# Self attention of a perceiver block: heads scored in row tiles of 32 rows, two heads sharing their output rows, the norm of q and k by query tile with GpSimd, half of the first output product early

## The reference

```python
x = x + cross(layernorm(x), ctx) @ W_out.T
h = layernorm(x)
q, k, v = split(h @ w_qkv.T + b_qkv)            # 16 heads of 16 columns each
q = q * rsqrt(mean(q * q) + 1e-6) * qn_w        # for each head
k = k * rsqrt(mean(k * k) + 1e-6) * kn_w
attn = softmax(q @ k.T / 4)                     # for each head, 256 x 256
x = x + (attn @ v) @ w_proj.T + b_proj
```

## Time and profile before

| | |
|---|---|
| median of 3 runs | 748.99 us (747.96 to 749.51) |
| the profiled execution | 750.28 us |
| its span, first to last instruction | 748.6 us |
| mean granted TensorE clock | 0.963 |
| TensorE products busy | 646.4 us (86%), 4972 instructions |
| TensorE weight loads busy | 390.7 us (52%) |
| VectorE busy | 413.4 us (55%) |
| ScalarE busy | 464.5 us (62%) |
| GpSimd busy | 71.9 us (10%) |

### The profile page before, as it was taken

How to read it: one execution, slowest core, us unless ns; L and a number is a source line. 1 busy time by engine, 2 the same in 40 slices (tenths; PEclk the granted TensorE clock), 3 DMA queues, 4 the chain that set the end, 5 groups by cost and what they waited for, 6 DMA issues and landing times. The chain is left out here.

```text
span 748.6 us, 14468 instructions
## 1 busy us (share of the span) xinstructions
PE 646.4 (86%) x4972; PEld 390.7 (52%) x4972; DVE 413.4 (55%) x903; ACT 464.5 (62%) x558; POOL 71.9 (10%) x148
## 2 busy tenths in 40 slices
PE   1698777878788769898589999999999899988997
PEld 1354444444445345575235555555555567754886
DVE  6576352231322315865578898988883426446443
ACT  3899969999999974472036676767767046303100
POOL 3010201000100003000110101111110200000000
PEclk9999979999999999999758999999999999999899
DMA  5787765384433114000802332323230740000000
GB/s 132 217 245 212 232 205 168 105 239 152 143 112 109 49 25 151 1 1 0 287 9 72 86 81 76 88 79 84 77 83 2 241 139 1 2 0 1 0 1 14
DMA packets 52694, 73.39 MB, mean 98 GB/s; under 512 B 10866, under 2 KB 29618, under 8 KB 52658
## 3 DMA queue, kind: packets, MB, share of 16 engines
q1 hardware_dynamic: 51890, 72.19, 33.0%
q10 hardware_dynamic: 768, 0.73, 0.3%
HBM read 58.89 MB, written 12.85 MB: 96 GB/s over the span
## 5 line engine op out<-in xcount | busy, mean ns | idle before, releaser
L1575 DVE TENSOR_REDUCE sb_m_blk<-ps 128x1 f32<-128x512 f32 x256 | 159.6, 683 | 22.8 <-PE ps L1432 21.7
L1383 ACT ACTIVATE sb_probs<-ps 128x1024 f32<-128x1024 f32 x128 | 125.9, 1025 | 52.9 <-PE ps L1462 51.7
L651 ACT ACTIVATE sb_probs<-ps 128x1024 f32<-128x1024 f32 x128 | 124.0, 1016 | 16.5 <-PE ps L697 14.2
L655 ACT ACTIVATE sb_probs<-sb_probs,sb_neg_cap,sb_cap 128x4096 f32<-128x4096 f32 x32 | 121.6, 3801 | 1.1
L714 PE MATMUL ps<-sb_probs,sb_v_st 128*32 128x256 f32 x1024 | 77.5, 400 | 41.1 <-ACT sb_probs L655 38.7
L1432 PE MATMUL ps<-sb_k_st,sb_q_m 96*128 96x512 bf16 x256 | 91.4, 402 | 2.7 <-DVE sb_m_blk L1575 2.0
L697 PE MATMUL ps<-sb_q_st,sb_k_st 112*128 112x256 bf16 x512 | 76.6, 285 | 5.9 <-DMA sb_k_st<-k_parts_l 4.2
L1462 PE MATMUL ps<-sb_q_st,sb_k_st 115*128 115x256 bf16 x512 | 77.7, 275 | 1.4 <-ACT sb_probs L1383 1.4
L697 PEld LDWEIGHTS ps<-sb_q_st,sb_k_st 112*128 112x128 bf16 x512 | 46.2, 101 | 49.7 <-ACT sb_probs L651 23.8
L1478 PE MATMUL ps<-sb_probs,sb_v_st 128*32 128x256 f32 x1024 | 67.7, 385 | 0.2 <-ACT sb_probs L1383 0.2
L714 PEld LDWEIGHTS ps<-sb_probs,sb_v_st 128*32 128x32 f32 x1024 | 24.2, 110 | 70.4 <-ACT sb_probs L655 49.3
(11 more groups left out here) (264 smaller groups left out, 875.0 us busy)
## 6 DMA issues: line engine op xcount, KB each, us to landing
sb_k_st<-k_parts_l SPq DMA_DIRECT2D x223, 64.0 KB, 2.0
sb_k_st<-k_parts_l SPq DMA_DIRECT2D x93, 128.0 KB, 3.2
k_parts_l<-sb_v_proj SPq DMA_DIRECT2D x24, 256.0 KB
k_parts_l<-sb_early SPq DMA_DIRECT2D x48, 128.0 KB
sb_v_proj<-ctxT_blocks SPq DMA_DIRECT2D x8, 512.0 KB, 8.9
sb_early<-ctxT SPq DMA_DIRECT2D x7, 512.0 KB, 4.0
sb_v_rows<-ctx_by_pair SPq DMA_DIRECT2D x7, 512.0 KB, 3.9
sb_k_st<-k_parts_l SPq DMA_DIRECT2D x64, 32.0 KB, 1.8
```

The lines of the kernel that those rows point to most:

```text
L651: a.activation(probs[:, j % 2, 4 * g:4 * g + 4, :], scores_bank(g), ACT.Tanh).then_inc(s["tanh"], 1)
L655: a.activation(probs[:, j % 2], probs[:, j % 2], ACT.Exp, bias=k.neg_cap[:, 0:1], scale=k.cap[:, 0:1]).then_inc(s["exp"], 1)
L1383: sc.activation(probs[:, g], scores_bank(g), ACT.Exp).then_inc(s["exp"], 1)
L1575: v.tensor_reduce(k.m_blk[:, b, q, blk:blk + 1], k.ps[:, m_bank(m_turn_of(idx)), :], AX.X, ALU.max).then_inc(s["m_read"], 1)
```

## The change

Five parts, and what follows from them.

1. In `stage_cross0`, before the last value products, TensorE turns the first half of `o_nat` and multiplies it by the first half of the weights; VectorE copies the turned half. The stage after does the second half only and adds to the same banks. The ternary weights' absolute sum goes from the self attention to VectorE's list here. Two `keep_busy` products of 256 columns are added.
2. q and k are handled for each query tile by itself (bias, square, sum, product). GpSimd multiplies by the norm weights beside the chain. The ternary scaling goes ahead of the bias on VectorE, the second mask row behind the squares on ScalarE.
3. A head's scores use the 32 rows that hold it and its neighbour. `q_par` holds q twice, once with the odd heads' rows zero and once with the even heads' (two masked copies instead of sixteen). A pair is now heads h and h + 2, in different row tiles, and their scores go to different banks.
4. In `v_self` odd heads fill columns 16 to 31 and even heads columns 0 to 15, and both add to the same 32 output rows (`joined`), so the result fills one bank, and the output product goes over two blocks.
5. `w_proj0` is loaded in one transfer, without zero rows; the memset for them and SyncE's wait for it go.

```diff
@@ stage_cross0: tensor, vector
                 body(it, False)
+            pe.wait_ge(s["o_read"], H - 1)
+            for q in range(QT):
+                last = t.transpose(k.ps[:, 4, q * P:(q + 1) * P], k.o_nat[:, q, 0:P], k.ident[:, :])
+            last.then_inc(k.sem("a_oT_ps"), 1)
+            pe.wait_ge(k.sem("a_oT"), 1)
+            pe.wait_ge(s["v_copied"], H)
+            pe.wait_ge(k.sem("w2_in"), 16 * W2_LOADS)
+            for q in range(QT):
+                t.matmul(k.ps[:, 6 + q, 0:D], k.oT[:, 0, q * P:(q + 1) * P], k.w_out0[:, 0, :], start=True, stop=False)
             for c in range(4):
                 pv(H // 2 - 1, 3, c, False)
+            keep_busy(k, 1, 1, D)
             sel(H - 1, 1)
+            keep_busy(k, 1, 1, D)
...
+            dve.wait_ge(k.sem("a_oT_ps"), 1)
+            v.tensor_copy(k.oT[:, 0, :], k.ps[:, 4, 0:S]).then_inc(k.sem("a_oT"), 1)
+            dve.wait_ge(k.sem("w2_in"), 16 * W2_LOADS)
+            v.tensor_reduce(k.w_sum[:, :], k.w_ffn0[:, :, :].rearrange("p t n -> p (t n)"), AX.X, ALU.add,
+                            apply_absolute_value=True).then_inc(k.sem("c_w_sum"), 1)
             copy_acc(H - 1, 1)
@@ Small
+    def edges(self, h, c, tiles):
+        return c == 0 and not (self.joined and h % 2), c == tiles - 1 and not (self.joined and h % 2 == 0)
@@ stage_self0
-    att = Small(k, H, False,
-                q_of=lambda h, q: k.q_mask[:, h, q * P:(q + 1) * P],
-                k_of=lambda h, nk: k.kT_self[:, h // 8, 0:nk],
+    quad = lambda h: slice(32 * (h // 2 % 4), 32 * (h // 2 % 4) + 32)
+    att = Small(k, [((h, h + 2), q) for h0 in range(0, H, 4) for q in range(QT) for h in (h0, h0 + 1)], False,
+                q_of=lambda h, q: k.q_par[quad(h), h % 2, h // 8, q * P:(q + 1) * P],
+                k_of=lambda h, nk: k.kT_self[quad(h), h // 8, 0:nk],
                 v_of=lambda h, c: k.v_self[:, c, h, :],
...
+                out_of=lambda h, q, r: k.ps[quad(h), 4, h // 8 * S + q * P:h // 8 * S + (q + 1) * P],
+                scores=lambda n: k.ps[:, 2 * (n % 2):2 * (n % 2) + 2, 0:S],
+                turned=lambda n: k.ps[:, 6 + n % 2, :], joined=True)
@@ stage_self0: gpsimd (behind the two memsets, which stay)
+            for q in range(QT):
+                pool.wait_ge(k.sem("b_qk_rows"), q + 1)
+                heads = lambda a: a[:, q, :].rearrange("p (s h d) -> p s h d", s=2, d=DH)
+                nc.gpsimd.tensor_tensor(heads(k.qk_w), heads(k.qk), k.w_qkn[:, :, :].unsqueeze(2).to_broadcast([P, 2, H, DH]),
+                                        ALU.mult).then_inc(k.sem("b_qk_w"), 1)
@@ stage_self0: tensor
-            update_pe(k, pe, "a", k.oT, KT, k.w_out0, True)
+            for q in range(QT):
+                last = t.transpose(k.ps[:, 0, q * P:(q + 1) * P], k.o_nat[:, q, P:2 * P], k.ident[:, :])
+            last.then_inc(k.sem("a_oT_ps"), 1)
+            keep_busy(k, 1, 1, D)
+            pe.wait_ge(k.sem("a_oT"), 2)
+            for q in range(QT):
+                last = t.matmul(k.ps[:, 6 + q, 0:D], k.oT[:, 1, q * P:(q + 1) * P], k.w_out0[:, 1, :], start=False, stop=True)
+            last.then_inc(k.sem("a_y"), 1)
+            keep_busy(k, 5, 1)
...
+            keep_busy(k, 3, 6)
             for q in range(QT):
+                pe.wait_ge(k.sem("b_qkn"), q + 1)
...
+            keep_busy(k, 1, 7, D)
+            pe.wait_ge(k.sem("b_qkT_in"), 3)
+            pe.wait_ge(k.sem("b_v_in"), 2)
             small_pe(k, pe, att)
-            update_pe(k, pe, "b", k.oT_pad, 4, k.w_proj0, False, norm=False)
+            update_pe(k, pe, "b", k.oT, KT, k.w_proj0, False, norm=False)
@@ stage_self0: scalar
             act.wait_ge(k.sem("d_mask_in"), 16)
+            mask_rows(0)
             for q in range(QT):
+                act.wait_ge(k.sem("b_qk_rows"), q + 1)
+                sc.activation(k.qk_sq[:, q, :], k.qk[:, q, :], ACT.Square).then_inc(k.sem("b_sq"), 1)
+            mask_rows(1)
             act.wait_ge(k.sem("b_qkT"), 1)
-            for h in range(8, H):
-                sc.activation(k.q_mask[:, h, :], k.ps[:, 2, 0:S], ACT.Copy, scale=k.head_mask[:, h - 8:h - 7]).then_inc(k.sem("b_qm_act"), 1)
+            sc.activation(k.q_par[:, 0].rearrange("p c q -> p (c q)"), k.ps[:, 0, :], ACT.Copy, scale=k.par_mask[:, 0:1]).then_inc(k.sem("b_qkT_in"), 1)
@@ stage_self0: vector, behind the copy of the turned rows
+            vec.tensor_scalar(k.w_qkn[:, 0, :], k.w_qkn[:, 0, :], 1.0 / np.sqrt(DH), None, ALU.mult).then_inc(k.sem("b_w"), 1)
+            dve.wait_ge(k.sem("c_w_total"), 1)
...
+            for q in range(QT):
+                dve.wait_ge(k.sem("b_qk"), q + 1)
+                vec.tensor_tensor(k.qk[:, q, :], k.ps[:, 3 + q, :], k.b_qkv0[:, 0:2 * D], ALU.add).then_inc(k.sem("b_qk_rows"), 1)
+            for q in range(QT):
+                dve.wait_ge(k.sem("b_sq"), q + 1)
+                link(vec.tensor_reduce(k.rs_v[:, 2 * H * q:2 * H * (q + 1)], k.qk_sq[:, q, :].rearrange("p (h d) -> p h d", d=DH), AX.X, ALU.add))
+            link(vec.tensor_scalar(k.rs_v[:, :], k.rs_v[:, :], 1.0 / DH, 1e-6, ALU.mult, ALU.add))
+            rsqrt(k, link, 64)
+            for q in range(QT):
+                dve.wait_ge(k.sem("b_qk_w"), q + 1)
+                vec.tensor_tensor(heads(k.qk), heads(k.qk_w), k.rs_y[:, 2 * H * q:2 * H * (q + 1)].unsqueeze(2).to_broadcast([P, 2 * H, DH]),
+                                  ALU.mult).then_inc(k.sem("b_qkn"), 1)
...
-            for h in range(8):
-                vec.tensor_scalar(k.q_mask[:, h, :], k.ps[:, 0, 0:S], k.head_mask[:, h:h + 1], None, ALU.mult).then_inc(k.sem("b_qm_dve"), 1)
+            dve.wait_ge(k.sem("b_qkT_in"), 2)
+            vec.tensor_scalar(k.q_par[:, 1].rearrange("p c q -> p (c q)"), k.ps[:, 0, :], k.par_mask[:, 1:2], None, ALU.mult).then_inc(k.sem("b_qkT_in"), 1)
...
-            vec.tensor_copy(k.oT_pad[:, :, :].rearrange("p (b g) q -> p b (g q)", b=2), k.ps[:, 4:6, :]).then_inc(k.sem("b_oT"), 1)
+            vec.tensor_copy(k.oT[:, :, :].rearrange("p c q -> p (c q)"), k.ps[:, 4, :]).then_inc(k.sem("b_oT"), 1)
```

More of the change, by code:

```diff
@@ L987, in scores @@
     def scores(n):
-        h0, q = a.pairs[n]
+        heads, q = a.pairs[n]
         nk = a.tiles(q) * P
@@ L991, in scores @@
             pe.wait_ge(s["exp"], 2 * (a.base + n - 1))
-        for e in range(2):
-            o = k.ps[:, n % 2, e * S:e * S + nk]
-            last = t.matmul(o, a.q_of(h0 + e, q), a.k_of(h0 + e, nk), start=True, stop=not a.causal)
+        for e, h in enumerate(heads):
+            o = a.scores(n)[:, e, 0:nk]
+            last = t.matmul(o, a.q_of(h, q), a.k_of(h, nk), start=True, stop=not a.causal)
             if a.causal:
@@ L999, in turn @@
     def turn(n):
-        h0, q = a.pairs[n]
+        q = a.pairs[n][1]
         pe.wait_ge(s["pn"], 2 * (a.base + n + 1))
@@ L1043, in copy_turned @@
         sc.activation(k.sp_T[:, n % 2, :].rearrange("p (e m) -> p e m", e=2)[:, :, 0:nk],
-                      k.ps[:, 2 + n % 2, :].rearrange("p (e m) -> p e m", e=2)[:, :, 0:nk], ACT.Copy).then_inc(s["PT_copied"], 1)
-    for n, (h0, q) in enumerate(a.pairs):
+                      a.turned(n).rearrange("p (e m) -> p e m", e=2)[:, :, 0:nk], ACT.Copy).then_inc(s["PT_copied"], 1)
+    for n, (_, q) in enumerate(a.pairs):
         nk = a.tiles(q) * P
@@ L1051, in small_act @@
         for e in range(2):
-            sc.activation(k.sp_rows[:, n % 2, e, 0:nk], k.ps[:, n % 2, e * S:e * S + nk], ACT.Exp,
+            sc.activation(k.sp_rows[:, n % 2, e, 0:nk], a.scores(n)[:, e, 0:nk], ACT.Exp,
                           bias=k.nmax[:, 2 * n + e:2 * n + e + 1],
@@ L1185, in _ @@
[L1185 to L1192 removed]
+            dve.wait_ge(k.sem("a_oT_ps"), 2)
@@ L1671, in stage_self1 @@
     v, sc, t = nc.vector, nc.scalar, nc.tensor
-    causal = Small(k, 2 * E_T, True,
+    by_two = lambda heads: [((h, h + 1), q) for h in range(0, heads, 2) for q in range(QT)]
+    one_bank = lambda n: k.ps[:, n % 2, :].rearrange("p (e m) -> p e m", e=2)
+    turned = lambda n: k.ps[:, 2 + n % 2, :]
+    causal = Small(k, by_two(2 * E_T), True,
                    q_of=lambda h, q: k.e_qT[:, h // 2, q * P:(q + 1) * P],
```

122 lines of the change are left out of this document (53 added, 69 removed).

## The result

The change made the kernel slower: 758.94 us, median of 4 runs (754.69 to 761.31), against 748.76 before (4 runs, 747.96 to 749.51); ratio 1.0127, 95% interval 1.0085 to 1.017: a small loss, but clear of the noise. The profiled execution took 757.73 us, its span 756.0. The forecast was 738.2. What came true is the rival called *Slower*, which had been priced at 761 and given a chance of 0.03.

What follows compares the result with a forecast made beforehand. TensorE was taken to bound the head loop, a chain hopping between engines the run-up. Terms +0.4 + 0 - 6.7 + 1.2 + 0.4 - 3.9 - 2.2 = -10.8 on the 748.99 median gave 738.2 us; range 735.0 to 742.5.

Steps and rivals of the forecast that it cites:

- Slower: Rival for the head loop: clock stays at 0.5, period 3.2, 761 us if for all sixteen pairs; chance 0.03.
- Part 1: Early half of the first output product: value products 0.4 us late (+0.4); the norm waits for GpSimd's memset, so gain 0.
- Port free: Rival at the norm's start: the 1.01 us tensor_scalar isn't waiting for the memset; 733.1 us; chance 0.10.
- Part 2: From the turned rows' copy to the first scores: 18.25 us shrinks to 11.55, -6.7 us.
- The clock: Half-clock losses before the first scores: +1.2 us at the qkv products, +0.4 (0 to 1.2) for the later gap.
- Part 3: Head loop: paired scores overlap (-0.43), tile-shape switch costs 0.15; period 2.06 becomes 1.79, -3.9 us in all.
- Scores one after another: Rival for the head loop: the two row tiles don't overlap, loop +2.1, 744.2 us; chance 0.10.
- Partial overlap: Rival for the head loop: only the middle two records overlap, three slots for four, loop -1.0, 741.1 us; chance 0.08.
- Part 4: Behind the loop: smaller copy (-0.5) and eight output-product records instead of sixteen (-1.7), -2.2 us.
- a loop at 0.5: Sign that would show the forecast wrong: the head loop running at a granted clock of 0.5.
- 25 us as the point from which it decides: Head loop: half clock, +1.4 us a period, decides the result once it lasts over some 25 us.

Runs made afterwards that it cites:

- e6: e1 with the 3 x 8192 memset moved from GpSimd to ScalarE at the block's start; 733.8 us, ratio 0.9798 to the kernel before.
- e7: e6 without the early half of the first output product; 740.4 us, ratio 0.9904 to the kernel before.
- e8: e1 without the early half of the first output product; 742.8 us, ratio 0.9918 to the kernel before.
- e1: Changed kernel plus filler products at the head loop's start: three of 256 columns, short ones around the first two pairs' turns; 738.6 us, ratio 0.9853.
- e4: Changed kernel with both heads of a pair read from the same 32 rows, so scores can't overlap (timing only); 769.0 us, ratio 1.0247.
- e11: Changed kernel with only three filler products of 256 columns between the second and third scores; 743.0 us, ratio 0.9912 to the kernel before.
- e3: Changed kernel with the scores' operands over all 128 rows instead of 32 (timing only); 743.4 us, ratio 0.9925 to the kernel before.
- e10: Changed kernel with four filler products of 512 columns once, at pair 6, nothing at the loop's start; 756.4 us, ratio 1.0112.
- e12: e1 with two idle VectorE reductions ahead of pair 6's normalisation, forcing a TensorE gap; 758.0 us, ratio 1.0102 to the kernel before.
- e13: e3 with two idle VectorE reductions forcing a TensorE gap at pair 6 (timing only); 754.5 us, ratio 1.006 to the kernel before.
- e2: Changed kernel with one filler product of 128 columns ahead of each pair's turn, nothing at the loop's start; 764.1 us, ratio 1.0184.

## Why the prediction was wrong

- **Part 1, +0.4 and 0: right.** Value products at 276.00 behind an Exp that starts at 271.87, 4.13, against 3.85 before; X +0.33. The wait for the memset grew to 4.03 us, and e6 shows that it is a wait. The Trainium skill (SBUF — State Buffer, "Who interferes with whom") has a VectorE instruction in a two-port mode and a GpSimd instruction exclude each other; the 4.03 us and e6 agree, though no run shows in which mode the instruction ran. So *Port free* is out.
- **Part 2, -6.7: right.** e6, e7 and e8, where the clock is full, have 11.54 from X to the first scores; the forecast was 11.55. GpSimd's products took 1.27 us instead of 1.09 and were still hidden.
- **The clock, +1.2 and +0.4: right up to the first scores.** qkv products at half from 291.4, first scores at X + 13.04 where 13.15 was the sum. It varies with no change to the code there: 14.27 in e1 and 14.58 in e4, 3.0 above the 11.54 at full clock, where the bounds of the two terms allow 2.9.
- **Part 3's mechanism: right.** Period 1.79 at full clock, overlap 0.42 (forecast 0.43) and 0.15 for scores on 32 rows measured one by one; the loop of e11 is 4.18 shorter than before's, forecast 3.9. *Scores one after another* is out, and *Partial overlap* too. The Trainium skill (TensorE: Matmul & The Clock Gate, Part 3) has matmuls kept in strict order of start and end, from which three slots and a period of 2.0 were worked out; the trace, with 1.79, disagrees with that reading. It doesn't say which record is whose head's, so the order itself stays untested.
- **Part 4, -2.2: right**, -2.27.
- **The step that failed** is the loop's term. "-3.9" took the granted clock in the loop as 1.00 and the sum has no term for it; measured is +14.49, at 0.50 for 44.4 us. It was left out on the strength of the sentence "Against: before, the loop ran whole at 1.00", which also gave the last rival its 0.03. That row is of 128-row products. I let it speak for 32-row ones, and counted busy microseconds, which is where e3 and e4 are equal and their clocks are not. Two smaller faults led there. I looked for gaps ahead of the first scores and not behind them, though the shorter scores had to widen that one: 0.97 before, 1.41 after. (Filling that gap is enough to hold the loop at full clock, as e11 shows, but in e4 and e10 the clock fell ahead of it, so the gap isn't the whole cause.) And I priced a fall as a stretch that ends by itself (0 to 1.2 us), because every fall in the trace of before did. The rival's price was near: thirteen periods of +1.42 are 18.5, and after's loop is 18.7 longer than e11's; 761 against 758.9.

Every term of the sum but the clock's was within 0.3 us of what the runs show for it at full clock, and the result was off by 20.7. Of these, 18.4 are the loop's (14.49 + 3.9), by a term that the sum didn't have; the rest is the difference between the profiled executions and the medians. Two sentences of the prediction ("a loop at 0.5" as what would show it wrong, and 25 us as the point from which it decides; it lasted 44.4) located the danger; the chance of 0.03 didn't weigh it.

## What to carry to other kernels

Before a change takes work from a dense TensorE loop, ask what holds its clock, and take the rows that the products use into account, not only busy time. At the loop's start fill the waits of TensorE that are there anyway: three filler products of 256 columns in a 1.4 us wait turned 1.3% slower into 0.9% faster (e11; 1.5% in e1, which had a few more and whose loop is 0.85 us longer: the difference lies behind the loop). And when a step in front of a GpSimd instruction gets earlier, look for what now waits for its end: moving the memset to an idle ScalarE was worth another 4 us up to X.

## What the runs showed of the hardware that I had not expected

- This loop, with scores on 32 rows, has two lasting states: 1.79 and 3.21 us a pair, same instructions; a 5.2 us burst of full-row work lifts it (e10), an 8.6 us gap drops it (e12), and left alone it stays (after: 44.40 us busy without a break at 0.50).
- Rows count. With both at half clock and hardly any idle time, the loop with scores on 128 rows won it back within 4.0 us (e13), the one with scores on 32 rows didn't in 25.8 (e12), and won it back 3.2 to 4.9 us behind its last scores (after, e2, e4, e12). The Trainium skill (TensorE: Matmul & The Clock Gate, Part 1) ties the clock to how busy the engine has been, and doesn't speak of rows; by busy time alone after's loop should have come back, and the trace disagrees.
- A little full-row work in a half-clock loop isn't enough: e2's 0.43 us in each 3.74 only made it longer.
- Scores on 32 rows, with the switch of tile shape to the turns, cost 0.15 us a pair at full clock (2.21 against 2.06), and two heads on different row tiles and banks overlapped fully: 0.42 of the expected 0.43.
